# Switch experts, two 16-head attentions and two relu layers in one block, with the gathered batches taken inside the first attention's first tiles

## What is computed

```python
# fourth: 32 switch experts, one per token, room for 80 tokens in each
slot = where(accepted, top1 * C + pos, E * C)
buf = zeros(...).at[slot].set(xt)
y = einsum(silu(buf @ w_gate) * (buf @ w_up), w_down)
out_tok = where(accepted, y[slot] * gate, 0.0)
x = layernorm(x + (xt + out_tok))
# fifth: attention over groups of 32 tokens, relu layer, reorder, attention, relu layer
x = _mha(x, la_...)      # 16 heads, softmax(q k / 8) v - v, projection, layernorm with g, b
x = _ffn(x, lf_...)      # layernorm(relu(x @ w1 + b1) @ w2 + b2 + x)
x = _mha(reordered x, sa_...)
x = _ffn(x, pf_...)
```

## Time and profile before

| | |
|---|---|
| median of 3 runs | 1851.13 us (1848.86 to 1851.44) |
| the profiled execution's own time | 1853.07 us |
| its span in the trace | 1851.2 us |
| TensorE busy | 1537.6 us (83%) |
| VectorE busy | 1013.3 us (55%) |
| ScalarE busy | 868.2 us (47%) |
| GpSimd busy | 632.8 us (34%) |
| mean granted clock of TensorE | 0.905 of full speed |

### The profile page before, as it was taken

One profiled execution on the slowest core, in us unless ns is written; L12 is line 12 of the kernel. 1 busy time (PEld: TensorE's weight loads), 2 busy tenths in 40 slices (PEclk: granted clock), 3 DMA queues, 4 the chain that ended last, 5 costly groups with the idle time before them and its releaser, 6 DMA issues. The chain is left out here.

```text
span 1851.2 us, 31581 instructions
## 1 busy us (share of the span) xinstructions
PE 1537.6 (83%) x11326; PEld 1136.8 (61%) x11327; DVE 1013.3 (55%) x2402; ACT 868.2 (47%) x1935; POOL 632.8 (34%) x707
## 2 busy tenths in 40 slices
PE   4689977899787999995669999999974895668996
PEld 3356664566573577764647878787763774535664
DVE  6565546665376799982245553566452221344555
ACT  5556544555357777752434444444441231235553
POOL 3487513976132577753210001000036005111113
PEclk8799988899896899996869999999986898869998
DMA  7300000000002444706160000000001102100000
GB/s 221 102 13 12 12 7 3 12 18 12 7 1 38 80 75 78 79 22 165 42 186 1 1 1 1 1 1 0 1 1 46 29 19 46 11 4 2 2 2 24
DMA packets 75277, 63.71 MB, mean 34 GB/s; under 512 B 25367, under 2 KB 62790, under 8 KB 75142
## 3 DMA queue, kind: packets, MB, share of 16 engines
q1 hardware_dynamic: 65142, 53.53, 13.0%
q0 software_dynamic: 3072, 6.30, 1.7%
q10 hardware_dynamic: 6928, 2.12, 0.5%
HBM read 48.09 MB, written 9.57 MB: 31 GB/s over the span
## 5 line engine op out<-in xcount | busy, mean ns | idle before, releaser
L1354 POOL TENSOR_TENSOR inject<-delta_x,b_rows 128x512 f32<-128x512 f32 x128 | 159.6, 1270 | 82.7 <-DVE delta_x L1604 42.2
L1625 DVE TENSOR_TENSOR_SCAN state<-bank,inject 128x512 f32<-128x512 f32 x128 | 150.4, 1206 | 5.0 <-ACT bank L1535 4.7
L2058 POOL TENSOR_TENSOR ve<-mv,eps 128x1 f32<-128x1 f32 x32 | 6.1, 190 | 341.3 <-DVE mv L2206 341.3
L1535 ACT ACTIVATE bank<-delta,a_neg 128x255 f32<-128x255 f32 x256 | 109.0, 472 | 11.9 <-DVE state L1625 11.4
L3313 DVE TENSOR_REDUCE top<-bank 128x2 f32<-128x512 f32 (+1 forms) x96 | 61.8, 686 | 72.4 <-PE bank L3015 51.5
L2167 ACT ACTIVATE Z<-bank 128x512 f32<-128x512 f32 x64 | 34.7, 595 | 129.4 <-PE bank L2120 129.4
L2762 DVE TENSOR_TENSOR shared_hid<-shared_gate,bank 128x256 f32<-128x256 f32 x64 | 26.5, 421 | 124.9 <-ACT shared_gate L2674 72.6
L2144 ACT ACTIVATE U<-bank 128x512 f32<-128x512 f32 x128 | 74.6, 593 | 40.3 <-PE bank L2081 39.2
L2618 PE MATMUL bank<-xT,sg 128*128 128x256 f32 x128 | 45.3, 437 | 55.8 <-DVE shared_hid L2762 51.3
L594 POOL TENSOR_TENSOR rotated<-rot_cos,rot_sin 128x512 f32<-128x512 f32 x56 | 70.8, 1268 | 52.2 <-DVE rot_sin L900 52.2
L600 POOL TENSOR_TENSOR inv_norm<-sum_sq,neghalf 128x16 f32<-128x16 f32 x28 | 82.0, 2929 | 4.2 <-POOL sum_sq L598 0.2
(11 more groups left out here) (564 smaller groups left out, 4205.1 us busy)
## 6 DMA issues: line engine op xcount, KB each, us to landing
b_rows<-b_rows_dram SPq DMA_DIRECT2D x32, 512.0 KB, 8.6
v<-v SPq DMA_DIRECT2D x32, 130.0 KB, 2.3
slots<-zero SPq DMA_DIRECT2D x10, 256.0 KB, 3.6
rows<-slots SPq DMA_DIRECT2D x10, 256.0 KB, 4.7
moe_w<-in_L_ffn_rg_dram SPq DMA_DIRECT2D x1, 2048.0 KB, 8.6
moe_w<-in_L_ffn_ru_dram SPq DMA_DIRECT2D x1, 2048.0 KB, 14.3
wqkv<-in_L_ffn_wqkv_dram SPq DMA_DIRECT2D x2, 768.0 KB
slots_out<-y SPq DMA_DIRECT2D x8, 160.0 KB, 2.1
```

The source lines that it names most:

```text
L1354: pool.tensor_tensor(dB[:, n % R, :, :], dx[:, :, seq(n)], both(b_all[:, q % 4, n % CH, :]), ALU.mult).then_inc(s.inject.sem, 1)
L1535: last = act.activation(dA[n % RD][:, c, 1:L], delta[:, c, i * L + 1:(i + 1) * L], ACT.Exp, scale=a_neg[:, c, k:k + 1])
L1625: dve.tensor_tensor_scan(flat(h[:, n % R, :, :]), flat(dA[n % RD]), flat(dB[:, n % R, :, :]), 0.0, ALU.mult, ALU.add).then_inc(s.state.sem, 1)
```

## The change

The two stages become one block, `experts_and_second_layer`. The boundary between them (barrier, clearing of signals, opening) goes; the block opens 82 signals at the start of the experts, with 22 semaphores more, and ends with one more barrier that clears these. The attention's buffers are cut out of the experts' rooms that are free by then (`places`, `tables`, `passing`, `y`), so the names in the trace change with them.

VectorE combines batches 0 to 2 before the attention (`combined(dve, 0, 1, 2)`, which normalises batches 0 and 1), batches 3 and 4 behind tile 0's transposed probabilities, 5 and 6 behind tile 1's, 7 behind tile 2's. TensorE turns batch 0 before the attention and each other batch behind an item of the ring. From batch 2 on GpSimd makes the reciprocal deviation, behind its gathers, in place of ScalarE's root and VectorE's reciprocal. Each tile's `load_x` waits for its batch alone.

```diff
+        BACK = {1: 1, 8: 2, 9: 3, 13: 4, 14: 5, 19: 6, 20: 7}
...
+        def turned_back(pe, k):
+            pe.wait_ge(s.x_updated.sem, s.x_updated.at(0, min(2 * k + 4, B)))
...
+            if i < 2:
+                dve.wait_ge(s.root.sem, s.root.at(0, i + 1))
+                dve.reciprocal(rstd[:, of], root[:, of]).then_inc(s.rstd.sem, 1)
+                dve.wait_ge(s.rstd.sem, s.rstd.at(0, i + 1))
+            else:
+                dve.wait_ge(s.pool_rstd.sem, s.pool_rstd.at(0, i - 1))
+                dve.wait_ge(s.xnT_ready.sem, s.xnT_ready.at(0, i - 1))
...
+        def combined(dve, *batches):
+            for i in batches:
+                combine(dve, i)
+                if i >= 1:
+                    normalise(dve, i - 1)
+                statistics(dve, i)
+
+        def back_on_vector(dve, k):
+            if k < 2:
+                combined(dve, 3 + 2 * k, 4 + 2 * k)
+            elif k == 2:
+                combined(dve, 7)
+                normalise(dve, 7)
...
+            for i in {0: (2, 3, 4, 5, 6), 1: (7,)}.get(k, ()):
+                of = slice(TPB * i, TPB * (i + 1))
+                pool.wait_ge(s.agg.sem, s.agg.at(0, i + 1))
+                pool.tensor_tensor(root[:, of], mv[:, of, 1], net.eps[:, 0:TPB], ALU.add).then_inc(s.var_eps.sem, 1)
+                pool.wait_ge(s.var_eps.sem, s.var_eps.at(0, i - 1))
+                pool.tensor_tensor(rstd[:, of], root[:, of], net.neghalf[:, 0:TPB], ALU.pow).then_inc(s.pool_rstd.sem, 1)
...
+        def x_ready(act, first, k):
+            act.wait_ge(s.x_updated.sem, s.x_updated.at(0, k // 2 + 1 if first else B))
...
+                turn_back(pe, 0)
+                la.begin_tensor(pe)
...
+                combined(dve, 0, 1, 2)
+                la.on_vector(dve)
...
+                sp.wait_ge(s.agg.sem, s.agg.at(0, B))
                 with nc.allow_non_contiguous_dma(reason="biases, one to a partition, and a small router"):
                     for to, of, done in load:
                         sp.dma_start(to, of).then_inc(done, 16)
...
+        nc.all_engine_barrier(sems_to_clear=range(extra[0].num, extra[0].num + len(extra)))
     close_stage(nc, net.pool)
```

More of the change, by code:

```diff
@@ L2054, in on_gpsimd, with turn @@
     def on_gpsimd(pool):
-        with pool.Fori(0, TURNS) as i:
+        def turn(i, first, last):
             for k in range(K):
+                if first:
+                    behind_pool(pool, k)
                 pool.wait_ge(s.agg.sem, s.agg.at(i, k + 1))
@@ new lines, in experts_and_second_layer @@
+        moved, stored = net.moved, net.stored
+        plain = lambda ap: ap.rearrange("d h k -> d (h k)")
+        given = [ap for ap, *_ in net.loads2[0:10]]
+        heads = [(plain(q), plain(k), plain(v), p) for q, k, v, p, _ in (given[0:5], given[5:10])]
+        by_head = lambda ap: ap.rearrange("p (h d) -> p h d", d=D)
+        scores_w = [(by_head(q), by_head(k)) for q, k, v, p in heads]
+        values_w = [(by_head(v), p) for q, k, v, p in heads]
+        w_res = [net.zero[:, m * D:(m + 1) * D] for m in range(2)]
@@ new lines, in norms @@
+        def norms(room):
+            n_st, n_mv, n_ve, n_rstd = cut(room, NT * 6, NT * 2, NT, NT)
+            return group(st=two(n_st, 6), mv=two(n_mv, 2), ve=n_ve, rstd=n_rstd)
+        relu_rooms = group(xb=two(xb_, L), hid=hid_.rearrange("p (k c t) -> p k c t", k=2, c=C), xn=mxn_.rearrange("p (k t d) -> p k t d", k=2, t=TPB),
+                           x0=two(x0_, L), z=two(z_, L), sq=two(places[:, 0:2 * P], P), own=norms(own_), end=norms(end_))
+        pb_la, pb_sa = net.zero[:, 2 * D:3 * D], net.zero[:, 3 * D:4 * D]
@@ L2461, in second_layer @@
         counted = {k: v for k, v in s_lf._asdict().items() if not k.startswith(("end_", "x0_", "z_", "squares"))}
[L2462 to L2465 removed]
+        s_pf = s_lf._replace(**{k: v.behind(1) for k, v in counted.items()})._replace(b2_ps=s_all.b2_ps, b2=s_all.b2)
@@ new lines, in experts_and_second_layer, with turn_back, deviation @@
+        nothing = lambda eng, n=0: None
+        BACK = {1: 1, 8: 2, 9: 3, 13: 4, 14: 5, 19: 6, 20: 7}
+        def turn_back(pe, i):
+            pe.wait_ge(s.xn_ready.sem, s.xn_ready.at(0, i + 1))
+            if i >= 2:
+                pe.wait_ge(s.x_updated.sem, s.x_updated.at(0, i - 1))
+            for t in range(TPB):
+                last = pe.transpose(bank[6 + i % 2][:, t * P:(t + 1) * P], xn[:, i % 2, t, :], net.tab("ident"))
+            last.then_inc(s.xnT_ready.sem, 1)
+        def deviation(act, i):
+            act.wait_ge(s.agg.sem, s.agg.at(0, i + 1))
+            act.activation(root[:, TPB * i:TPB * (i + 1)], mv[:, TPB * i:TPB * (i + 1), 1], ACT.Sqrt, bias=net.eps[:, 0:1]).then_inc(s.root.sem, 1)
@@ L2539, in stage_relu_mlp @@
         (first, second), (between, end) = net.attentions, net.mlps
-        second_layer(nc, net, first, between, second, end)
+        experts_and_second_layer(nc, net, first, between, second, end)
 def stage_top2_experts(nc, net, io):
```

601 lines of the change are left out of this document (290 added, 311 removed).

## The result

The change is slower: **1858.34 us** (median of 6, 1856.79 to 1860.90) against 1850.61 us of before (6 runs beside them); ratio **1.0046**, 95% interval 1.0033 to 1.0059, so 7.7 us lost where 5.6 gained were forecast. The profiled execution took 1858.43 us, its span is 1856.5 us.

The account below looks back on a forecast made before the run. Free engines in the gather's tail and the attention's head, then TensorE from tile 2 on. Lead 7.4 at tile 2, less 1.2 (opening) and 0.6 (barrier), gains 5.6 us: 1845.5 against 1851.13, range 1841.5 to 1851.5.

Parts of the forecast that it names:

- part 1: Start of tile 0: attention waits only for batch 0, scores at 930.4 instead of 952.96, a lead of 22.5 us.
- the lead at tile 2: Tile 2's value products come at 974.7 instead of 982.10, 7.4 us sooner than in the kernel before.
- part 2: Tile 0 pays for batches 2 to 4: value products at 941.8 against 960.29, lead down to 18.5 us.
- part 3: Tile 1 pays for batches 5 and 6: value products at 959.0 against 971.79, lead down to 12.8 us.
- part 4: Tile 2 pays for batch 7: value products at 974.7 against 982.10, lead down to 7.4 us.
- part 5: Merged block's cost elsewhere: experts open 1.2 us later, one more barrier at the end costs 0.6 us.
- VectorE's pause falls into the open chain: Rival: VectorE's pause near 933.53 hits tile 0's softmax, lead down by 3.3 us, 1848.8 us; chance 0.15.
- slower rival: TensorE's clock stays at half through tiles 1 and 2, costing 9.9 us, 1855.4 us; chance 0.07.
- A premise: Behind tile 2's value products nothing waits for batches, so the lead there is kept to the end.

Follow-up runs that it names:

- r3: The change itself, unaltered, run again in the fourth series; 1767.76 us, ratio 0.9982 to the kernel before.
- f1: The change, but GpSimd issues the gathers of batches 3 to 7 only when tile 0's scores are done; 1851.54 us, ratio 0.9996 to the kernel before.
- r2: The change itself, unaltered, run again in the third series; 1860.24 us, ratio 1.0032 to the kernel before.
- r1: The kernel before, unaltered, run again for its trace in the third series; 1849.94 us.
- e8: The change with 44 unused transpositions on TensorE ahead of the turns of batches 2, 4, 6 and 7; 1856.84 us, ratio 1.0020 to the kernel before.
- g1: Against the change: four batches combined ahead of the attention, gathers of 4 to 7 issued after tile 0's scores; 1754.02 us, ratio 0.9903 to the kernel before.
- g0: g1 without GpSimd's pause, all gathers issued in one row; 1753.92 us, ratio 0.9911 to the kernel before.
- The third and the fourth series: Sets of runs on one chip each: r1, r2, e8, f1 (kernel before 1852.4 us), and g0, g1, g2, r3 (kernel before 1770.6 us).
- e3: Against the change: batches 0 to 4 combined ahead of tile 0's softmax, 5 to 7 turned in the sum's bank; 1843.32 us, ratio 0.9962 to the kernel before.
- e7: e3 with batch 4 turned behind tile 1's third weight group, batch 7 one weight group earlier; 1751.56 us, ratio 0.9881 to the kernel before.
- g2: e7 again, unaltered, in the fourth series; 1751.81 us, ratio 0.9884 to the kernel before.

## Why the prediction was wrong

The step that failed is part 1, through a thing that the sum did not hold: the stand, which put tile 0's scores 7.3 us later. It decided the sign: without it the ratio is 0.9982 (r3) or 0.9996 (f1). In the sum's own terms, the lead at tile 2 was forecast at 7.4 and measured at -4.8, 12.2 lower. Part 1 is 6.3 of this, part 2 is 1.8, part 3 is 2.5 and part 4 is 1.6; part 5 adds 0.4. And where there is no stand (r3), the gain was 2.9 us and not 5.6, so about half of the forecast gain is missing even there.

- **Part 1 failed.** It read tile 0's ring as 6.83 us of TensorE work and took ScalarE's copies between as free to follow. In the change they fall beside GpSimd's gathers, and in the kind of series in which both kernels were measured ScalarE stands there. Tile 0's scores came 19.8 us behind the first combine instead of the 13.3 of the forecast (930.4 - 917.06), and 12.4 in r3 and 12.7 in f1, without the stand. I had read the trace of before for this place only, where the stand was VectorE's (2.2 us at 933.53); the 24.5 us at L2666 in the same trace, on ScalarE, was the row that would have warned of it.
- **Rival "VectorE's pause falls into the open chain"** had the right kind of cause and the wrong engine: I asked whether the pause belongs to the moment, and it does, but the engine that works in that moment now is ScalarE, and behind it stand TensorE, the scores and tile 0's whole softmax. It paid 7.3 us (19.8 - 12.4), not 3.3. The Trainium skill (SBUF — State Buffer, Who interferes with whom) ties only VectorE and GpSimd together and says that ScalarE never waits on anyone at that port; the stand of 7.5 us in r2 and its end by the pause of f1 show ScalarE held beside GpSimd's transfers all the same, so that rule is not its cause. Nor is TensorE spared (r1's group at 1405.56 above).
- **Part 2** was right in its terms: from scores to value products 11.3 us in r3, 11.4 in the forecast (941.8 - 930.4). In the change it took 13.1: after the stand TensorE's scores ran at half clock (1.93 instead of 1.06).
- **Parts 3 and 4** were undersized. From one tile's value products to the next it took 19.2 and 16.4 us in r3; the forecast had 17.2 and 15.7. The projections with their residual took 5.1 and 5.5 us, not 4.3 and 4.5, and tile 0's value products (2.62 us) and tile 1's scores (1.94) ran at half clock too. With the stand it was 19.7 and 17.3, the projections 6.3 and 6.2 (963.73 to 970.07, 981.19 to 987.35) with the clock at 0.50 to 0.53 in the windows above. This is the **slower rival's** mechanism. It priced the two projections at 3.5 and 3.3 us above the forecast's 4.3 and 4.5; they came 2.0 and 1.7 above in the change, and 0.8 and 1.0 above in r3. Filling TensorE's wait brought tile 1's projection back to full clock (e8: tile 2's value products at 68.9 instead of 70.8). The mechanism is real, but r3 has about half of it and is faster than before, so it isn't what decided the sign.
- **The lead against before** was too high by another 2.0 us for r3: before's tile 2 comes 2.0 us sooner in a series without stands (63.0 for 65.0). This bears on r3 alone; in the result both kernels have their stands. Hence 7.4 forecast, 3.7 measured in r3 (1.7 us from the change, 2.0 from before).
- **Part 5**: first scatter behind the opening 14.0 us instead of 12.8, so 1.2 as forecast; another 1.0 came until the gathers, in the kind with stands, where ScalarE stands beside the scatters too. Without them it was 71.6 against 70.7 in all. End of the program: from VectorE's last normalisation (1852.09, 1847.08) to the span's end 4.4 against 4.1, where 0.6 more was forecast; from tile 2's value products to the end the two traces are equal, so this 0.3 isn't seen in the whole.
- **A premise** of the prediction, that whatever lead there is at tile 2 is kept by all that follows, holds for this pair of traces (869.1 us behind it in both) and fails in others: g1 makes good, by the clock, the 5.2 us by which it is behind g0 at tile 3.
- **The account** in the kind measured: 3.7 (r3's lead), less 7.3 for the stand itself, less 3.2 for half clock and longer waits behind it, plus 2.0 for before's own stands is -4.8, the lead in the trace; less 2.2 at the opening: 7.0 us slower, the difference of the traces.

What stays open: what holds the engines. The stands come only beside or just behind rows of indirect transfers and only in some series. The third and the fourth series carry the same chip number and fall on different sides, so I can't put it down to the chip. A late transfer of instructions is neither shown nor excluded: the records have two queues of instruction transfers, which aren't named by engine, and neither carries anything between 904.2 and 938.2 in the change (nor between 892.2 and 919.5 in r3, which has no stand).

## What to carry to other kernels

Before work is moved beside another engine's transfers, look in the *whole* trace for instructions that start long after their inputs and ask what ran at that time: such a stand costs nothing where it is covered, and lands in the path when the move opens the chain. Fill the idle engine first and put the rest where a wait for it holds nobody: e3 and e7 moved the same batches as the change, five instead of three ahead of the softmax and the turns out of the value products' banks. e3 won 0.4 per cent with stands, and e7's order 1.0 to 1.2 per cent without them. And measure a change of 0.3 per cent in more than one series: here its sign depended on the series.

## What the runs showed of the hardware

- The same program (before) takes 1851 us or 1770 us by the series. In the slower kind ScalarE stands up to 34.4 us at an instruction whose inputs are there, beside rows of 16 or 32 indirect transfers, and TensorE up to 2.2 us at single matmuls (r1, 1428.00). Rows of 6 and 10 gathers with a pause between them (f1) brought no stand of ScalarE.
- One program, e7, g2 and h2: from the opening to the first combine 76.9, 72.3 and 76.9 us. The difference lies in the experts' products, at half clock in one and at full clock in the other. Windows of e7, then of g2:

```profile
880.00:884.00 4.00, 4.00 (x20) 4.00 (x20) 0.49 (x1) 0.87 (x2) 0.00 (x0) 0.50 0.01 4
```

```profile
880.00:884.00 4.00, 4.00 (x37) 4.00 (x38) 0.69 (x2) 1.95 (x3) 0.00 (x0) 1.00 0.02 4
```

These 4.6 us are more than the change itself is worth in r3 (2.9 us), and they come and go between executions.
